# The opening of the first attention: TensorE centres and turns the cross pass's key and query weights, x is taken in pairs, and transfers are split by chunk of heads

## The reference

```python
ln_out = _ln(hidden_states, ln_w, ln_b)
q = _ln(_fp8_linear_pertensor(ln_out, wq, wq_scale, q_in_scale).reshape(b, s, g, hpg, d), qln_w, qln_b)
...
qx = _fp8_linear_pertensor(ln_out, wqx, wqx_scale, qx_in_scale).reshape(b, s, g, hpg, d)
qx = _ln(qx, qxln_w, qxln_b)
kvx = jnp.einsum('bsi,oi->bso', cond, w_kv_x)
kx, vx = jnp.split(kvx, 2, axis=-1)
kx = _ln(kx.reshape(b, sc, g, d), kxln_w, kxln_b)
xout = _gqa(qx, kx, vx).reshape(b, s, nh * d)
...
return jnp.einsum('bsi,oi->bso', catq, wproj) * (proj_in_scale * proj_w_scale)
```

## Time and profile before

| what | value |
|---|---|
| median of 3 runs | 1510.41 us (1510.2 to 1511.01) |
| the profiled execution's own time | 1510.13 us |
| its span | 1508.3 us |
| TensorE matmul busy | 1430.7 us (95%) |
| VectorE busy | 891.3 us (59%) |
| ScalarE busy | 768.1 us (51%) |
| GpSimd busy | 528.0 us (35%) |
| mean granted TensorE clock | 0.992 |

### The profile page before, as it was taken

The page is one execution under the profiler, slowest core; times in us unless marked ns, Lnnn a source line. Parts: engine busy times, 40 slices in busy tenths (PEclk is TensorE's granted clock), DMA queues, the critical chain, the costliest instruction groups (busy, mean ns, idle before and its releaser), DMA issues. The chain is left out here.

```text
span 1508.3 us, 22223 instructions
## 1 busy us (share of the span) xinstructions
PE 1430.7 (95%) x6910; PEld 1028.8 (68%) x6910; DVE 891.3 (59%) x1934; ACT 768.1 (51%) x2122; POOL 528.0 (35%) x519
## 2 busy tenths in 40 slices
PE   3999998999989999999999999999997999999998
PEld 1678777788875556557878888876764666665656
DVE  7898988898975342323454545354677555553322
ACT  4888888899973211110234444444457555554210
POOL 2667577877762000000434242422110333331000
PEclk9999999999999999999999999999999999999999
DMA  5211000200005511112100000000232000011120
GB/s 202 73 51 60 8 5 2 96 2 1 2 1 220 217 51 51 54 49 91 67 1 1 1 1 1 15 15 1 107 143 102 1 1 1 1 30 42 46 68 18
DMA packets 21303, 71.65 MB, mean 48 GB/s; under 512 B 3858, under 2 KB 6290, under 8 KB 18244
## 3 DMA queue, kind: packets, MB, share of 16 engines
q1 hardware_dynamic: 12980, 57.37, 10.2%
q10 hardware_dynamic: 8208, 12.87, 2.7%
HBM read 69.01 MB, written 1.22 MB: 47 GB/s over the span
## 5 line engine op out<-in xcount | busy, mean ns | idle before, releaser
L1189 ACT ACTIVATE l0f_silu<-bank 128x512 f32<-128x512 f32 x48 | 28.5, 597 | 199.8 <-PE bank L1113 189.7
L827 POOL TENSOR_TENSOR l0a_stepped<-l0a_y,l0a_m 128x512 f32<-128x512 bf16 x64 | 73.9, 1154 | 91.5 <-DVE l0a_m L575 90.4
L1292 DVE TENSOR_TENSOR l0f_product<-l0f_silu,bank 128x512 f32<-128x512 f32 x48 | 32.9, 688 | 123.4 <-ACT l0f_silu L1189 123.3
L855 POOL TENSOR_TENSOR l0a_head_rstd<-l0a_head_var,all_minus_half 128x4 f32<-128x4 f32 x96 | 99.7, 1043 | 7.6 <-DVE l0a_head_var L597 7.6
L767 ACT ACTIVATE l0a_work<-bank,l0a_neg_max 128x128 f32<-128x128 f32 x256 | 90.2, 370 | 1.0 <-DVE l0a_neg_max L610 0.9
L1125 PEld LDWEIGHTS bank<-all_weights_a,l0f_hidden 128*128 128x128 f32 x384 | 72.9, 190 | 25.2 <-issue 17.0
L1721 DVE TENSOR_TENSOR all_weights_a<-bank,all_cols 128x512 f32<-128x512 f32 x64 | 43.9, 690 | 77.9 <-PE bank L1556 45.9
L427 PEld LDWEIGHTS bank<-l0a_k_t,l0a_q_t 128*128 128x128 f32 x512 | 64.0, 191 | 36.7 <-ACT l0a_q_t L753 31.3
L1125 PE MATMUL bank<-all_weights_a,l0f_hidden 128*128 128x256 f32 x384 | 88.9, 379 | 0.0
L2314 PE MATMUL bank<-l3a_f_xn_t,all_weights_b 128*128 128x512 f32 x192 | 86.2, 593 | 0.0
L800 ACT ACTIVATE l0a_work<-l0a_work,l0a_row_inv 128x128 f32<-128x128 f32 x256 | 82.3, 409 | 6.8 <-DVE l0a_row_inv L614 6.7
(11 more groups left out here) (437 smaller groups left out, 3754.1 us busy)
## 6 DMA issues: line engine op xcount, KB each, us to landing
l0f_spread<-l0f_weights ACTq DMA_DIRECT2D x32, 192.0 KB, 2.7
all_weights_a<-in_l_w_q SPq DMA_DIRECT2D x2, 2048.0 KB, 14.3
l0f_spread<-l0f_weights ACTq DMA_DIRECT2D x32, 128.0 KB, 2.8
all_weights_b<-in_l_e_gate_up SPq DMA_DIRECT2D x1, 3200.0 KB, 10.3
all_weights_b<-in_l_e_gate SPq DMA_DIRECT2D x1, 3072.0 KB, 10.0
all_weights_a<-in_l_e_up SPq DMA_DIRECT2D x4, 768.0 KB, 7.0
all_weights_a<-in_l_e_down SPq DMA_DIRECT2D x1, 3072.0 KB, 15.4
l3a_spread<-l3f_weights SPq DMA_DIRECT2D x10, 256.0 KB, 3.5
```

Of the source, the lines that this page charges most:

```text
L827: done = g.tensor_tensor(stepped[:, 0:n], value, step, ALU.add)
L855: g.tensor_tensor(head_rstd[:, m % 2, :], head_var[:, m % 2, :], res.minus_half[:, 0:HU], ALU.pow)\
```

## The change

TensorE now centres and turns the raw weights of the cross pass's keys and queries in one multiplication for each head and half of the inputs: the weights are stored the other way round in HBM (outputs on the partitions), and are multiplied with `centring`, the identity less 1/128. There are 2 chunks of keys and 4 of queries, 8 multiplications of 128x128 f32 each. The product lies in PSUM; ScalarE copies it from there (`keep_kx`, and `high` with the scale), VectorE takes the low part from there. VectorE's `centre` of these chunks is gone.

x is taken in four pairs of tiles, each with its own semaphore, moments, power, rows, turning and copy. The key and query weights come in transfers of a chunk each, 512 KB. The raw key weights lie in `wvx`, so that the value weights can only be loaded when both key chunks are centred: SyncE waits for that (`kx_centred`), then issues the value weights, and behind them `raw_p`.

```diff
+        centring = mem.sb("centring", [P])
...
         raw_q, raw_p = view(res.wb, 0, KC, 2048), view(res.wb, 4096, 16, D)
+        raw_qx = view(res.wb, 0, 16, D)
+        raw_kx = wvx[:, :, :].rearrange("p c (h n) -> p (c h) n", n=D)
...
+        KX_BANKS = [res.banks[4:6], res.banks[6:8]]
+        QX_BANKS = [res.banks[4:6], res.banks[6:8], res.banks[5:7], res.banks[6:8]]
+        LN_BANKS = [res.banks[1], res.banks[2], res.banks[3], res.banks[1]]
...
-            for t in range(0, TILES, 2):
-                sp.dma_start(res.x[:, t:t + 2, :], w["x"][:, t:t + 2, :]).then_inc(x_in, 16)
+            for p in range(XPAIRS):
+                sp.dma_start(res.x[:, 2 * p:2 * p + 2, :], w["x"][:, 2 * p:2 * p + 2, :]).then_inc(x_in[p], 16)
+            sp.dma_start(raw_kx[:, 0:4, :], w["l0_w_kx"][:, 0:4, :]).then_inc(kx_in[0], 16)
             sp.dma_start(ctx_t[:], w["ctx_t"][0]).then_inc(ctx_in, 16)
-            sp.dma_start(wkx[:], w["l0_w_kx"]).then_inc(kv_loaded["k"], 16)
-            sp.dma_start(raw_q, w["l0_w_qx"]).then_inc(q_loaded, 16)
-            sp.dma_start(wvx[:], w["l0_w_vx"]).then_inc(kv_loaded["v"], 16)
+            sp.dma_start(raw_qx[:, 0:4, :], w["l0_w_qx"][:, 0:4, :]).then_inc(qx_in[0], 16)
+            sp.dma_start(raw_kx[:, 4:8, :], w["l0_w_kx"][:, 4:8, :]).then_inc(kx_in[1], 16)
+            for u in range(1, 4):
+                sp.dma_start(raw_qx[:, 4 * u:4 * u + 4, :], w["l0_w_qx"][:, 4 * u:4 * u + 4, :]).then_inc(qx_in[u], 16)
+            sp.wait_ge(kx_centred, 2)
+            sp.dma_start(wvx[:], w["l0_w_vx"]).then_inc(vx_loaded, 16)
             sp.dma_start(raw_p, w["l0_w_proj_x"]).then_inc(p_loaded, 16)
...
+            def turn_x(p):
+                pe.wait_ge(rows_ready, p + 1)
+                if p == 3:
+                    pe.wait_ge(ln_ready, 1)
+                for i in range(2):
+                    for c in range(KC):
+                        at = (i * KC + c) * P
+                        mm = pe.transpose(LN_BANKS[p][:, at:at + P], rows[:, 2 * p + i, c * P:(c + 1) * P], res.ident[:])
+                mm.then_inc(rows_turned, 1)
+
+            def centre_heads(raw, u, banks):
+                for c in range(KC):
+                    for h in range(HU):
+                        mm = pe.matmul(banks[c][:, h * P:(h + 1) * P], raw[:, u * HU + h, c * P:(c + 1) * P], centring[:],
+                                       start=True, stop=True)
+                return mm
+
+            def centre_kx(u):
+                pe.wait_ge(kx_in[u], 16)
+                centre_heads(raw_kx, u, KX_BANKS[u]).then_inc(kx_centred, 1)
+
+            def centre_qx(u):
+                pe.wait_ge(qx_in[u], 16)
+                if u < 2:
+                    pe.wait_ge(kx_ready, u + 1)
+                else:
+                    pe.wait_ge(w_low, u)
+                centre_heads(raw_qx, u, QX_BANKS[u]).then_inc(qx_centred, 1)
+
+            def centre_first(k):
+                centre_qx(0)
+                centre_kx(1)
+
+            def centre_next(k):
+                centre_qx(k + 1)
+
             pe.wait_ge(cols_in, 48)
-            for t in range(TILES):
-                pe.wait_ge(rows_ready, t + 1)
-                if t >= 2:
-                    pe.wait_ge(ln_ready, t - 1)
-                for c in range(KC):
-                    mm = pe.transpose(proj_bank[t % 2][:, c * P:(c + 1) * P], rows[:, t, c * P:(c + 1) * P], res.ident[:])
-                mm.then_inc(rows_turned, 1)
-            pe.wait_ge(ln_ready, TILES)
+            pe.wait_ge(centring_ready, 1)
+            turn_x(0)
+            centre_kx(0)
+            for p in range(1, XPAIRS):
+                turn_x(p)
...
+                if G == 1:
+                    pe.wait_ge(ln_ready, XPAIRS)
...
-                        pe.wait_ge(kx_ready, 1)
+                        pe.wait_ge(kx_ready, u + 1)
                     else:
-                        pe.wait_ge(kv_loaded["v"], 16)
+                        pe.wait_ge(vx_loaded, 16)
...
+                               in_tile(0, centre_first, [0]), in_tile(0, centre_next, [1, 3, 5])])
...
+            def x_moments(p):
+                v.wait_ge(x_in[p], 16)
+                token_moments(v, res, res.x, [2 * p, 2 * p + 1])
+                pair = slice(2 * p, 2 * p + 2)
+                v.tensor_scalar(token_var[:, pair], res.moments[:, pair, 1], 1.0 + EPS, EPS * EPS, ALU.mult, ALU.add)\
+                 .then_inc(token_var_ready, 1)
+
+            def x_rows(p):
+                v.wait_ge(token_rstd_ready, p + 1)
+                for t in (2 * p, 2 * p + 1):
+                    done = v.tensor_scalar(rows[:, t, :], res.x[:, t, :], res.moments[:, t, 0:1], token_rstd[:, t:t + 1],
+                                           ALU.subtract, ALU.mult)
+                done.then_inc(rows_ready, 1)
+
+            x_moments(0)
+            v.tensor_scalar(centring[:], res.ident[:], 1.0 / P, None, ALU.subtract).then_inc(centring_ready, 1)
...
+            x_rows(0)
+            x_moments(1)
+            x_moments(2)
+            x_rows(1)
+            x_moments(3)
+            x_rows(2)
+            x_rows(3)
+            v.tensor_copy(res.ident16[:], res.ident[:])
...
-            kx_heads = wkx[:, :, :].rearrange("p c (h n) -> p (c h) n", n=P)
-            v.tensor_reduce(kx_mean[:].rearrange("p c h -> p (c h)"), kx_heads, X, ALU.add)
-            v.drain()
-            v.tensor_scalar(kx_mean[:], kx_mean[:], 1.0 / P, None, ALU.mult)
-            v.drain()
-            v.tensor_tensor(kx_heads, kx_heads, along(kx_mean[:].rearrange("p c h -> p (c h)"), P),
-                            ALU.subtract).then_inc(kx_ready, 1)
...
-                if kind == "v":
-                    v.wait_ge(kv_loaded["v"], 32)
+                if not core:
+                    for c in range(KC):
+                        done = v.scalar_tensor_tensor(wq[1][:, c, cols], QX_BANKS[u][c][:], in_scale[:, 0, c:c + 1],
+                                                      wq[0][:, c, cols].bitcast(F32), ALU.mult, ALU.subtract)
+                elif kind == "v":
...
-                if b == 0 and k % 2 == 0:
-                    if k // 2 < 3:
-                        centre(k // 2 + 1)
...
-            centre(0)
...
+            def keep_x(p):
+                act.wait_ge(rows_turned, p + 1)
                 for c in range(KC):
-                    done = act.activation(ln_t[:, c, t * P:(t + 1) * P], proj_bank[t % 2][:, c * P:(c + 1) * P],
+                    done = act.activation(ln_t[:, c, 2 * p * P:2 * (p + 1) * P].rearrange("p (i n) -> p i n", i=2),
+                                          LN_BANKS[p][:, :].rearrange("p (i c n) -> p i c n", i=2, c=KC)[:, :, c, :],
                                           ACT.Identity, scale=res.col("L0_xattn_ln_w", c), bias=res.col("L0_xattn_ln_b", c))
                 done.then_inc(ln_ready, 1)
-            act.wait_ge(scales_ready, 1)
+
+            def keep_kx(u):
+                act.wait_ge(kx_centred, u + 1)
+                for c in range(KC):
+                    done = act.activation(wkx[:, c, u * BANK:(u + 1) * BANK], KX_BANKS[u][c][:], ACT.Copy)
+                done.then_inc(kx_ready, 1)
...
+                    act.wait_ge(qx_centred, u + 1)
+                    for c in range(KC):
+                        done = act.activation(wq[0][:, c, cols], QX_BANKS[u][c][:], ACT.Copy, scale=in_scale[:, 0, c:c + 1])
...
+            keep_x(0)
+            act.wait_ge(scales_ready, 1)
+            act.wait_ge(ln_ready, 1)
             scale_input(-1, 0)
+            keep_kx(0)
+            for p in range(1, XPAIRS):
+                keep_x(p)
             high(0)
+            keep_kx(1)
+            act.wait_ge(ln_ready, XPAIRS)
+            act.wait_ge(affine_ready, 1)
...
-            g.wait_ge(token_var_ready, 1)
-            g.tensor_tensor(token_rstd[:], token_var[:], res.minus_half[:], ALU.pow).then_inc(token_rstd_ready, 1)
...
-    a["l0_w_qx"] = by_partition(i["L0_xattn_wqx"].T)
-    a["l0_w_kx"], a["l0_w_vx"] = (by_partition(half.T) for half in np.split(i["L0_xattn_w_kv_x"], 2))
+    a["l0_w_qx"] = by_partition(i["L0_xattn_wqx"])
+    w_kx, w_vx = np.split(i["L0_xattn_w_kv_x"], 2)
+    a["l0_w_kx"], a["l0_w_vx"] = by_partition(w_kx), by_partition(w_vx.T)
```

More of the change, by code:

```diff
@@ L248, in layer0_attention @@
         cols_in = mem.sem("cols_in")
-        x_in = mem.sem("x_in")
+        x_in = [mem.sem(f"x_in{p}") for p in range(TILES // 2)]
+        kx_in = [mem.sem(f"l0a_kx_in{u}") for u in range(2)]
+        qx_in = [mem.sem(f"l0a_qx_in{u}") for u in range(4)]
+        centring_ready = mem.sem("l0a_centring_ready")
+        kx_centred = mem.sem("l0a_kx_centred")
+        qx_centred = mem.sem("l0a_qx_centred")
         ready = mem.sem("constants_ready")
         scales_ready = mem.sem("l0a_scales_ready")
+        affine_ready = mem.sem("l0a_affine_ready")
+        vx_loaded = mem.sem("l0a_vx_loaded")
         kv_loaded = {k: mem.sem(f"l0a_raw_{k}_loaded") for k in "kv"}
@@ L532, in centre @@
```

(8 more changed lines are left out.)

40 lines of the change are left out of this document (18 added, 22 removed).

## The result

The changed kernel takes 1517.29 us (median of 5 runs, 1515.43 to 1518.44), the kernel before 1511.01 on the same occasions. The ratio is 1.004, with a 95% interval of 1.0028 to 1.0051: slower by 0.28 to 0.51%, 6.3 us between the medians. I had forecast 1517.5.

The account below looks back on a forecast made before the run. VectorE, centring weights, was taken to bound the opening, TensorE the rest. `raw_p` holding ScalarE until 31.4 plus 25.65 puts the mark at 57.05, 7.1 us later: span 1515.4, with 1.8 around it 1517.2, plus 0.3 gives 1517.5; range 1512.5 to 1520.5.

Parts of the forecast that it names:

- the mark: First turning of the probabilities on TensorE, from where it hardly waits: forecast 57.05 us against 49.95, 7.1 later.
- The second key chunk: Opening on TensorE: turnings, projection and centrings without a real gap, sum 13.2 us from 8.2, centred at 21.4.
- The price taken from L427: TensorE's centring of a chunk, from 4 multiplications in 1.05 us: 2.1 us at 2.4 GHz, double at 1.2 GHz.
- The landing: Transfers behind SyncE's wait: first 1 MB takes 5.1 us, each further one 2.5; `raw_p` is 2 MB, so 5.0 more.
- A: Time when ScalarE goes on with its first `out_high` after `raw_p` lands: 31.4 us, 7.0 behind the 24.42 of before.
- the interval: Time from A to the mark, three legs of the opening: 25.65 us, as long as the 25.5 of before.
- the leg: First leg, from A to the `high` of the third chunk: sum 12.05 us, with 2.6 for the centring of q2.
- The cold start: TensorE starts at 1.2 GHz after standing some 10 us; warm at once, the first leg would be 2.2 us shorter.
- the lag is made good: Rival for the opening: freed VectorE lets ScalarE run with half its waits, interval 21.3 us, 1513.2 us; chance 0.15.
- The rival that ends below the kernel before: Opening: ScalarE has no waits between first `out_high` and the mark, mark 4.15 us earlier, 1506.3 us; chance 0.08.
- the ring: Opening: each `high` needs TensorE's centring, which waits for the `low` before; about 7.7 us per chunk, before 7.3.
- The rival with TensorE cold through most of the opening: TensorE stays at 1.2 GHz through most of the opening and again later: +12.1 us, 1522.5 us; chance 0.12.

Follow-up runs that it names:

- TensorE kept at work: Changed kernel with 13 idle multiplications on TensorE between its projection of k1 and its first turning; ratio 1.0024 to the kernel before.
- `out_high` late: Changed kernel with ScalarE's four first-pass `out_high` moved to steps 4, 6, 8, 10 and GpSimd's low parts four steps later; ratio 0.9987 to the kernel before.
- key chunk 1 first: Changed kernel with the second key chunk centred on TensorE ahead of the projection of k0 and the centring of q0; ratio 1.0007 to the kernel before.
- the hold gone and the ring cut: Changed kernel with `raw_p` issued ahead of SyncE's wait and TensorE's centring one chunk ahead; 1504.5 us median, ratio 0.994 to the kernel before.

## Why the prediction was right

**The chain that was named is the one that happened.** ScalarE held by `raw_p`, 10.1 us (about 9 forecast); the first `out_high` at 32.22 (31.4); the mark at 57.47 (57.05), 7.5 us late (7.1). That the time came within 0.2 us (1517.29 for 1517.5) is luck beyond that: the medians are 6.3 us apart, not 7.1, and the kernel before took 1511.01 here, 0.6 more than the 1510.41 of the forecast.

**The parts of the sum, against what they measured.** The second key chunk was centred at 20.97, for 21.4: the cold centring took 3.40 us instead of 4.2, the warm ones 1.95 (the row at 17.24) instead of 2.1, and against it TensorE began at 8.6 instead of 8.2. The price taken from L427 was a little high, and double it more so. The landing: from the issue of the value weights 11.1 us, where I had 9.9. The value weights took 4.8 (5.1 forecast), but the 2 MB behind them 6.3 instead of 5.0. That was the largest error in a term, 1.3 us. With the key chunk 0.4 early and the landing 1.2 late, A came 0.8 late; the interval was 0.4 shorter than forecast, and the mark 0.4 late. The step with the error is the one that took 2.5 us for each further MB from transfers of 1 MB. It isn't a property of the size: with the same two issues one behind the other, `raw_p` landed after 10.7 and 10.5 us in the changed kernel and with TensorE kept at work, and after 9.4 in each of the runs with `out_high` late and key chunk 1 first. The last section shows where the 1.3 us lie. The estimate that I had worked out from the figures of the Trainium skill's page "DMA: Bandwidth & Descriptors" (sections "Latency and other measured facts" and "Where 436 GB/s comes from"), 9.2 us, would have been 1.9 short.

**From A to the mark.** Forecast 12.05 + 7.7 + 5.9; measured from 32.22 to the third `high` at 44.14, 11.9; to the fourth at 51.50, 7.4; to the mark, 6.0. The centring of q2 took 3.30, all of it cold, for 2.6; the leg was right since the work ahead of TensorE's turning took 6.0 us instead of 6.45. Here too two errors cancel.

**The cold start.** 2.2 forecast, 2.5 measured by keeping TensorE at work. The rule of the Trainium skill's page "TensorE: Matmul & The Clock Gate" (Part 1: The HAM clock gate), that idling throttles the array and work releases it, is borne out: the first four turnings after the stand took 1.11 us, and 0.66 with TensorE kept at work.

**The rivals.** That the lag is made good did not happen: the interval was 25.3, and not even the freed VectorE shortened it, because each `high` waits for TensorE. The rival that ends below the kernel before, ScalarE without waits, would have needed an interval of under 17.7 us from the measured 32.22 only to be level at the mark. With the hold gone and the ring cut it was 20.5. The rival with TensorE cold through most of the opening did not happen either: by the durations it was cold until 13.3, and the projection of k0 at 15.52 took 1.88 us.

**Where the expected gain went.** The change has one. With `raw_p` ahead of the wait it is 0.24%; without the pairs it is gone (0.9998), and the pairs on VectorE and GpSimd without the rest of the change have none that can be told from nothing (0.9994, an interval that holds 1). The change gave it away, and 0.4% more, by one transfer that stands behind a wait that it doesn't need: only the value weights need the place of the raw keys.

## What to carry to other kernels

When a transfer gets a new wait in its issuer's queue, look at what stands behind it in that queue, and then at what stands behind its consumer on the consumer's engine: the transfer that needs no wait belongs ahead of it. When work moves from a full engine to an idle one, see whether the new engine now lies in the ring from one chunk to the next; if so, let it run one chunk ahead. A long stand of the matmul engine costs more than its length: here the first 5.6 us of work after 11.5 us of standing ran at half the clock, for 2.5 us in all.
